# Mixture-of-experts FFN on one core: short last row blocks as float32 column groups, and a preamble in two chains

## The chip, the cores and the metric

One core of one Trainium2 chip runs the kernel. The metric is the time of one execution on the device, in microseconds; lower is better. Three runs of the kernel before took 217.95 us in the median (217.33 to 218.16).

## The reference

```python
def ffn_block(x, cond, q_right, gate, router_w, router_b, w1, b1, w2, b2):
    # r: x rotated by two normalised quaternions, one from cond and one from q_right,
    # and scaled by gate, column by column of the 4 x 64 quaternion parts
    r = hamilton(normalise(cond), hamilton(x * gate, conj(normalise(q_right))))
    logits = r @ router_w + router_b                    # (2048, 8)
    top1 = argmax(softmax(logits))
    out = zeros_like(r)
    for i in range(8):
        h = r @ w1[i] + b1[i]                           # 256 -> 2048
        a, g = split(h, 2)
        y = (a * sigmoid(g)) @ w2[i] + b2[i]            # 1024 -> 256
        out = out + where(top1 == i, y, 0)
    return x + out                                      # x: 8 x 256 tokens of 256 values, float32
```

The gate is constant along the sequence, so that the transform over tokens and its inverse cancel. Each token goes through one expert only. The kernel sorts the tokens by expert and computes each expert on its own tokens.

## The kernel before

**Tiles.** A tile is one expert with up to 512 of its tokens; up to three spare tiles take what is over 512 (none is used with these inputs). A tile is up to four blocks of 128 tokens. `SIZES` (L39) are the widths that the first product can have; each tile takes the smallest that holds its tokens, as a number in a table of control words, `ctrl`, which the kernel itself computes. The second product always computes whole blocks of 128 rows: two, three or four.

**Numbers.** Products are done in a faster 32-bit form, `fp32r`. Each operand is split into a high and a low part (ScalarE copies the high part, VectorE subtracts it from the value), and three products stand for one: high by high, high by low, low by high.

**The preamble.** TensorE turns x block by block (L912), ScalarE and VectorE copy the turned blocks out (L463, L656). VectorE builds the rotation matrix from the quaternions (L588 to L644). The logits are one product in four column groups of 32 columns (L929), with the router turned by the same rotation; ScalarE adds the bias (L485), TensorE turns them back (L949), VectorE finds each token's expert, its rank within the expert and from that its slot (L686 to L721). The counts over partitions are two small products on TensorE (L957, L958). Tables of one-hots (L723, L727) and 16 small products (L968) turn slots into lists of indices: `g_idx` for gathers and `s_idx` for scatters. Between these, TensorE rotates x (L941), ScalarE copies the rotated rows out (L491) and writes them to `x_rows` in DRAM in four DMAs of its own (L495). Then GpSimd gathers the first tile's rows, block by block (L363).

**Filler products** (`keep_warm`, L870, bf16; `keep_warm_long`, L875, float32) stand in places of the preamble where TensorE would otherwise have nothing to do. **Visits** are jumps to a place of TensorE's program that comes later and back.

**A tile.** TensorE turns the gathered rows (L987) at the end of the tile before; ScalarE and VectorE split them (L512, L759) and the tile's w1 in four units (L472, L665). The first product (L1029 to L1034) goes through eight pairs of 128 columns, g then a, in a ring of three pairs of PSUM banks. ScalarE makes the sigmoid (L524), VectorE the gated value into `u32` (L766, a ring of four) and sets `pair_free`, ScalarE and VectorE split that (L530, L772). The second product (L1049 to L1051) takes the blocks from the last to the first, each with 8 x 3 products of 256 columns, as soon as `u_lo_done` says that a part is there; it also waits for `w2_split`. VectorE adds the result to x + b2 in the next tile, after its third pair (L793), for the last tile at once (L801, L806). w2 is split after the third and fifth pair (L481, L670), in tile 0 ahead of them.

**Queues.** SyncE loads x, then w1 and w2 of the tile to come, each when its buffer has been split (L299 and L303). GpSimd issues, per tile and in this order, four gathers for the next tile, four scatters of the tile before and four fetches of x for the next one (L402 to L420).

## Time and profile before

| | us |
|---|---|
| median of three runs | 217.95 |
| profiled execution | 217.55 |
| its span, first to last instruction | 215.8 |
| start of the first expert product | 38.79 |
| TensorE busy | 205.6 |
| VectorE busy | 159.1 |
| ScalarE busy | 121.8 |
| GpSimd busy | 124.6 |
| bytes moved by DMA | 41.26 MB |

Busy times overlap, so that they don't add up. A timeline row gives the start, the duration, the engine, the line of the kernel, the operation with its tile and operands, how many instructions were merged, and in brackets the idle time before them with what ended it. The granted clock is given as a share of TensorE's full speed.

### The profile page before, as it was taken

How to read it: one execution, taken by the hardware profiler on the slowest of the kernel's cores; microseconds unless marked ns; L12 is line 12 of the kernel's file. 1: busy time of each engine (PE TensorE's matmuls, PEld its weight loads, DVE VectorE, ACT ScalarE, POOL GpSimd, SP SyncE). 2: the span in 40 equal slices, each digit the busy share in tenths (PEclk: the TensorE clock that was granted, in tenths of full speed). 3: DMA queues.
4: the chain of work that ended last, by engine and by line, in shares of the span. 5: the costliest groups of instructions: out<-in, count | busy, mean ns of one | idle time of the engine just before them, and what ended most of it. 6: DMA issues, size and time to landing. Idle time of an engine off the chain costs nothing.

```text
span 215.8 us, 4313 instructions
## 1 busy us (share of the span) xinstructions
PE 205.6 (95%) x1500; PEld 191.2 (89%) x1502; DVE 159.1 (74%) x307; ACT 121.8 (56%) x204; POOL 124.6 (58%) x146
## 2 busy tenths in 40 slices
PE   6986998899999999999999999999999999999992
PEld 3756843799999999999999999999999999999991
DVE  6826984877835999298969879994898469874960
ACT  2333692365916666386684958483949185745620
POOL 5000038776730788558878787887487818730751
PEclk9999999999999999999999999999999999999998
DMA  4995523799757173976499559837835692720011
GB/s 140 368 402 186 219 82 91 257 274 380 220 131 307 46 234 71 314 196 204 109 289 288 186 114 362 295 91 184 355 114 180 178 313 70 248 49 0 24 39 36
DMA packets 16964, 41.26 MB, mean 191 GB/s; under 512 B 2856, under 2 KB 11177, under 8 KB 14762
## 3 DMA queue, kind: packets, MB, share of 16 engines
q1 hardware_dynamic: 11490, 28.32, 36.7%
q0 software_dynamic: 4512, 10.50, 19.4%
q10 hardware_dynamic: 936, 2.17, 2.6%
q14 instruction: 19, 0.16, 0.2%
q8 instruction: 7, 0.11, 0.2%
HBM read 36.78 MB, written 6.03 MB: 198 GB/s over the span
## 4 chain that ended last, share of the span: by engine, by line
PE 67%; POOL 14%; issue 8%; DVE 5%; DMA 3%; ACT 1%; DVEq 0%; ACTq 0%; POOLq 0%
PE y_ps L1049 7%; PE y_ps L1051 7%; PE y_ps L1050 7%; PE g_ps L1029 5%; PE g_ps L1034 5%; PE g_ps L1030 5%; POOL out_dram L384 5%; PE a_ps L1029 5%; PE a_ps L1034 5%; PE a_ps L1030 5%; POOL y_out L375 5%; PE y_ps L870 3%; PE y_ps L875 3%; DMA xg<-x_rows,g_idx 3%; POOL xg L363 3%
## 5 line engine op out<-in xcount | busy, mean ns | idle before, releaser
L384 POOL DMA_INDIRECT out_dram<-y_out,s_idx x30 | 44.0, 1466 | 41.2 <-DVE y_out L793 30.4
L524 ACT ACTIVATE arena<-g_ps,b_t 128x384 f32<-128x384 f32 (+1 forms) x64 | 34.4, 538 | 48.2 <-PE g_ps L1034 48.2
L766 DVE SCALAR_TENSOR_TENSOR arena<-a_ps,b_t,arena 128x384 f32<-128x384 f32 (+1 forms) x64 | 36.0, 563 | 30.9 <-PE a_ps L1034 28.4
L363 POOL DMA_INDIRECT xg<-x_rows,g_idx x32 | 37.1, 1159 | 37.1 <-DVE g_idx L732 26.5
L1049 PE MATMUL y_ps<-w_hi,u_hi 128*128 128x256 f32 x168 | 48.5, 289 | 0.1
L1050 PE MATMUL y_ps<-w_lo,u_hi 128*128 128x256 f32 x168 | 47.5, 283 | 0.0
L1051 PE MATMUL y_ps<-w_hi,u_lo 128*128 128x256 f32 x168 | 47.5, 283 | 0.0
L375 POOL DMA_INDIRECT y_out<-in_x_dram,g_idx x32 | 40.3, 1259 | 9.8 <-issue 9.8
L665 DVE TENSOR_TENSOR w_lo<-w_raw,w_hi 128x1024 fp32r<-128x1024 f32 x32 | 37.3, 1221 | 4.7 <-DMA xg<-x_rows,g_idx 3.0
L530 ACT ACTIVATE u_hi<-arena 128x384 fp32r<-128x384 f32 (+1 forms) x64 | 30.7, 480 | 16.0 <-DVE arena L766 16.0
L1029 PE MATMUL g_ps<-xr_hi,w_hi 128*128 128x256 f32 (+3 forms) x128 | 37.0, 303 | 0.6 <-ACT xr_hi L512 0.6
L1029 PE MATMUL a_ps<-xr_hi,w_hi 128*128 128x256 f32 (+3 forms) x128 | 36.6, 299 | 0.0
L1030 PE MATMUL g_ps<-xr_hi,w_lo 128*128 128x256 f32 (+3 forms) x128 | 36.5, 299 | 0.0
L1030 PE MATMUL a_ps<-xr_hi,w_lo 128*128 128x256 f32 (+3 forms) x128 | 36.5, 299 | 0.0
L1049 PEld LDWEIGHTS y_ps<-w_hi,u_hi 128*128 128x128 f32 x168 | 32.2, 192 | 0.7 <-DVE u_lo L772 0.4
L772 DVE TENSOR_TENSOR u_lo<-arena,u_hi 128x384 fp32r<-128x384 f32 (+1 forms) x64 | 31.9, 499 | 1.2 <-ACT u_hi L530 0.3
L1050 PEld LDWEIGHTS y_ps<-w_lo,u_hi 128*128 128x128 f32 x168 | 32.2, 192 | 0.0
L1051 PEld LDWEIGHTS y_ps<-w_hi,u_lo 128*128 128x128 f32 x168 | 32.2, 192 | 0.0
L472 ACT ACTIVATE w_hi<-w_raw 128x1024 fp32r<-128x1024 f32 x32 | 31.2, 1057 | 0.5 <-ACT arena L491 0.5
L1034 PE MATMUL g_ps<-xr_lo,w_hi 128*128 128x256 f32 (+3 forms) x128 | 28.1, 300 | 0.0
L1034 PE MATMUL a_ps<-xr_lo,w_hi 128*128 128x256 f32 (+3 forms) x128 | 27.9, 299 | 0.0
L1029 PEld LDWEIGHTS g_ps<-xr_hi,w_hi 128*128 128x128 f32 x128 | 24.2, 189 | 1.3 <-issue 1.1
(150 smaller groups left out, 298.3 us busy)
## 6 DMA issues: line engine op xcount, KB each, us to landing
w_raw<-in_L_ffn_w_dram SPq DMA_DIRECT2D x16, 1024.0 KB, 8.9
w_raw<-in_L_ffn_w_dram SPq DMA_DIRECT2D x16, 512.0 KB, 5.0
arena<-in_x_dram SPq DMA_DIRECT2D x4, 512.0 KB, 6.2
x_rows<-arena ACTq DMA_DIRECT2D x4, 512.0 KB, 3.0
b_all<-in_L_ffn_b_dram SPq DMA_DIRECT2D x1, 1024.0 KB, 4.9
xg<-x_rows,g_idx POOLq DMA_INDIRECT x32, 7.1
y_out<-in_x_dram,g_idx POOLq DMA_INDIRECT x32, 4.5
out_dram<-y_out,s_idx POOLq DMA_INDIRECT x30
```

The costliest lines, as they stand in the source:

```text
L363: nc.gpsimd.indirect_dma_start(out=xg[:, s * DIM:(s + 1) * DIM], out_offset=None, in_=x_rows, in_offset=bass.IndirectOffsetOnAxis(ap=g_idx ...
L375: nc.gpsimd.indirect_dma_start(out=y_out[i % YB][:, s * DIM:(s + 1) * DIM], out_offset=None, in_=x_flat, in_offset=bass.IndirectOffsetOnAx ...
L384: nc.gpsimd.indirect_dma_start(out=out_flat, out_offset=bass.IndirectOffsetOnAxis(ap=s_idx[:, i * NSUB + s:i * NSUB + s + 1], axis=0), in_ ...
L524: nc.scalar.activation(sig[:, c % SIG_RING, 0:n], pair[c % RING][1][:, 0:n], ACT.Sigmoid, bias=b1_t[:, bass.ds(e * (2 * NC) + (NC + c), 1) ...
L665: V.tensor_tensor(unit_of(w1_lo, u), raw_unit(u), unit_of(w1_hi[:, :].bitcast(F32), u), ALU.subtract)\
L766: V.scalar_tensor_tensor(u32[:, c % (8 - SIG_RING), 0:n], pair[c % RING][0][:, 0:n], b1_t[:, bass.ds(e * (2 * NC) + c, 1)], sig[:, c % SIG ...
L1029: T.matmul(dst, w_part(w1_hi, k), xh, start=(k == 0), stop=False)
L1030: T.matmul(dst, w_part(w1_lo, k), xh, start=False, stop=False)
L1034: last = T.matmul(dst, w_part(w1_hi, k), xr_lo[:, k * ITEM:k * ITEM + n], start=False, stop=(k == KH - 1))
L1049: T.matmul(dst, u_hi[:, uv], w2_hi[:, wv], start=first, stop=False)
L1050: T.matmul(dst, u_hi[:, uv], w2_lo[:, wv], start=False, stop=False)
L1051: last = T.matmul(dst, u_lo[:, uv], w2_hi[:, wv], start=False, stop=final)
```

## The change

**Row blocks.** `SIZES` becomes (192, 256, 288, 320, 352, 512): 192 is new and 384 goes. Where the last block of a size holds 32 or 64 tokens (192, 288, 320), it is computed in float32 directly from `u32` and a whole, unsplit copy of w2, in column groups: the eight parts of the hidden dimension are dealt out to two groups of 64 or four groups of 32 columns of the array, each of which gathers its own partial sum. VectorE adds the groups afterwards, one small addition after the other, chosen by a branch on the tile's size. The first product is at least 256 wide. ScalarE and VectorE work on 256, 288, 320, 384 or 512 columns instead of whole blocks. `u32` now holds all eight parts and moves to the memory of the turned x. The whole w2 is a new load of SyncE, 1 MB per tile, behind the next tile's w1 (behind b2 for tile 0, and last of all for tile 7).

**Preamble.** The logits come in two halves, both before any rotation. A table of the spare tiles' places is made by GpSimd from the counts while VectorE computes the slots; the indices of the eight fixed tiles come first, those of the spare tiles after them in a second set of small products. The rotated rows are written by SyncE in eight DMAs of two row blocks. Half of w2 for tile 0 is loaded after them. The w2 split and the fourth w1 split of tile 0 go behind column pairs. Filler products become fewer, and the visits stand elsewhere. b1 and the gate are loaded by the other queue than before.

```diff
-    SIZES = (256, 288, 320, 352, 384, 512)
+    SIZES = (192, 256, 288, 320, 352, 512)
     BLOCKS = [(size + P - 1) // P for size in SIZES]
+    PARTS = {size: (size // P, size % P) for size in SIZES if size % P in (32, 64)}
...
+            def load_w2_whole(e):
+
+                if e > 0:
+                    sp.wait_ge(w2_whole_loaded, 16 * e)
+                    sp.wait_ge(mm2_done, e)
+                sp.dma_start(w2_whole, w2[e].rearrange("(c p) d -> p c d", p=P)).then_inc(w2_whole_loaded, 16)
...
+                if 1 < i < NE:
+                    load_w2_whole(i - 1)
...
-            for h in range(W2U):
-                load_w2(0, h)
-
+            x_rows_v = x_rows.rearrange("(p n) d -> p n d", p=P)
+            load_w2(0, 0)
+            for b in range(NB // 2):
+                sp.wait_ge(x_rot_done, b + 1)
+                sp.dma_start(x_rows_v[:, 2 * b:2 * b + 2, :], x_rot[:, 2 * b:2 * b + 2, :]).then_inc(x_rows_written, 16)
+            load_w2(0, 1)
             for s in range(NSUB):
                 sp.wait_ge(gathered[s], 16)
             sp.dma_start(b2_all[:, :], b2.rearrange("e d -> (e d)").partition_broadcast(P)).then_inc(b2_loaded, 16)
+            load_w2_whole(0)
             for e in range(1, NE):
                 load_tile(e, e)
+            load_w2_whole(NE - 1)
...
+            for m in range(SPARE):
+                last = G.tensor_single_scalar(over[:, m * NE:(m + 1) * NE], cnt, float((m + 1) * ITEM), ALU.is_gt)
+            link(last)
+            link(G.tensor_tensor(til, over[:, 0:NE], over[:, NE:2 * NE], ALU.add))
...
+            for half in (4 * NB, 2 * NB):
+                link(G.tensor_tensor(of_token[:, 0:half], of_token[:, 0:half], of_token[:, half:2 * half], ALU.add))
+            link(G.tensor_tensor(moved[:, :], of_token[:, 0:NB], of_token[:, NB:2 * NB], ALU.add))
+            pool.sem_inc(moved_ready, 1)
...
-            w2_hi_part(0)
...
-                if b % 2 == 1:
-                    act.wait_ge(x_rot_done, b + 1)
-                    act.dma_start(x_rows_v[:, 2 * b - 2:2 * b + 2, :], x_rot[:, 2 * b - 2:2 * b + 2, :])\
-                        .then_inc(x_rows_written, 16)
...
-            link(V.tensor_reduce(til, over, AX.X, ALU.add))
-            link(V.tensor_tensor_scan(spare_end, ones[:, 0:NE], til, 0.0, ALU.mult, ALU.add))
-            link(V.tensor_tensor(spare_from, spare_end, til, ALU.subtract))
-            link(V.scalar_tensor_tensor(delta, spare_from, float(ITEM), spare_at[:, :], ALU.mult, ALU.add))
-            link(V.scalar_tensor_tensor(ahead_en, pos_en, float(ITEM), delta.unsqueeze(2).to_broadcast([P, NE, NB]),
-                                        ALU.is_ge, ALU.mult))
-            link(V.tensor_tensor(pos[:, :], pos[:, :], ahead[:, :], ALU.add))
...
+            def add_parts(i, word, sizes_here):
+
+                def of_sizes(left):
+                    if not left:
+                        dve.sem_inc(dve_chain, more)
+                        return
+                    s, wide = PARTS[left[0]]
+                    with dve.If(f_size(word) == SIZES.index(left[0])):
+                        rows = y_out[i % YB][0:wide, s * DIM:(s + 1) * DIM]
+                        for g in range(1, P // wide):
+                            link(V.tensor_tensor(rows, y_ps[1][g * wide:(g + 1) * wide, PLACE[s] * DIM:(PLACE[s] + 1) * DIM],
+                                                 rows, ALU.add))
+                        if P // wide - 1 < more:
+                            dve.sem_inc(dve_chain, more + 1 - P // wide)
+                    with dve.Else():
+                        count[0] = start
+                        of_sizes(left[1:])
+
+                start = count[0]
+                more = max(P // wide for _, wide in PARTS.values()) - 1
+                of_sizes(sizes_here)
...
-                if i == 0:
-                    w1_lo_part(0, 3)
-                    w2_lo_part(0)
-                    dve.wait_ge(b2_loaded, 16)
-                elif i < NE:
+                if 0 < i < NE:
...
+                    if c == 1 and i == 0:
+                        w1_lo_part(0, 3)
                     if c == 2 and 0 < i < NE:
-                        add_rows(i - 1)
-                    if c == 4 and 0 < i < NE:
+                        add_rows(i - 1, word_before)
+                    if c == 4 and i < NE:
                         w2_lo_part(i)
                     if c == 4 and i + 1 < NE:
...
+            visit(1)
             pe.wait_ge(still_set, 1)
-            keep_warm(early_ps, 3)
-            visit(1)
+            keep_warm(early_ps, 5)
...
-            keep_warm(early_ps, 8)
-            visit(2)
+            keep_warm(early_ps, 5)
...
+            def logits(half):
+
+                for k in range(KH):
+                    tokens = x_t[:, k, half * 8 * P:(half + 1) * 8 * P].rearrange("p (j a t) -> p a j t", j=2, a=GROUPS)
+                    for a in range(GROUPS):
+                        last = T.matmul(xk_ps[half][a * COLS:(a + 1) * COLS, half * 2 * P:(half + 1) * 2 * P],
+                                        wr_rot[:, k * COLS:(k + 1) * COLS], tokens[:, a],
+                                        start=(k == 0), stop=(k == KH - 1))
+                last.then_inc(logits_t_ready, 1)
 
             pe.wait_ge(wr_ready, 1)
-            pe.wait_ge(x_t_done, 6)
-            pe.wait_ge(x_t_done_v, 2)
-            for k in range(KH):
-                for g in range(GROUPS):
-                    last = T.matmul(xk_ps[0][g * COLS:(g + 1) * COLS, :], wr_rot[:, k * COLS:(k + 1) * COLS],
-                                    x_t[:, k, g * 512:(g + 1) * 512], start=(k == 0), stop=(k == KH - 1))
-            last.then_inc(logits_t_ready, 1)
-            visit(3)
+            pe.wait_ge(x_t_done, 4)
+            logits(0)
+            pe.wait_ge(x_t_done, 7)
+            pe.wait_ge(x_t_done_v, 1)
+            logits(1)
...
+            for g in range(NB // GROUPS):
+                if g == 2:
+                    visit(3)
+                pe.wait_ge(logits_t_done, g // 2 + 1)
+                last = T.transpose(late_ps[:, g * P:(g + 1) * P], logits_t[:, g * P:(g + 1) * P], ident[:, :])
+            last.then_inc(logits_ready, 1)
+
             pe.wait_ge(rot_ready, KH)
-            rotate_blocks(0)
-            pe.wait_ge(logits_t_done, 1)
-            for j in range(NB // GROUPS):
-                last = T.transpose(late_ps[:, j * P:(j + 1) * P], logits_t[:, j * P:(j + 1) * P], ident[:, :])
-            last.then_inc(logits_ready, 1)
-
-            for b in range(1, 3):
+            for b in range(2):
                 rotate_blocks(b)
-            visit(4)
-            pe.wait_ge(consts_ready, 8)
+            pe.wait_ge(consts_ready, CONSTS)
...
+            for b in range(2, NB // 2):
                 rotate_blocks(b)
-
-            visit(5)
+                if b == 5:
+                    visit(4)
+            pe.wait_ge(b1_loaded, 16)
+            T.transpose(early_ps[:, 0:P], b1_rows[:, :], ident[:, :]).then_inc(b1_turned, 1)
+
+            landing(1)
...
             pe.wait_ge(b1_t_done, 1)
-            keep_warm(late_ps, 3)
             pe.wait_ge(q_oh_ready, 1)
             for n in range(NB):
                 pe.wait_ge(slots_ready, n + 1)
-                last = T.matmul(early_ps[:, 0:TS], slot_oh[:, n, :], q_oh[:, n * TS:(n + 1) * TS],
+                last = T.matmul(early_ps[:, 0:FX], slot_oh[:, n, :], q_oh[:, n * FX:(n + 1) * FX],
                                 start=(n == 0), stop=(n == NB - 1))
-                if n < NB - 2:
-                    keep_warm(late_ps, 1)
             last.then_inc(idx_summed, 1)
-            visit(6)
+            visit(5)
             pe.wait_ge(still32_set, 1)
-            keep_warm_long(late_ps, 5)
+            pe.wait_ge(q_oh_spare_ready, 1)
+            pe.wait_ge(x_rot_done, NB // 2)
+            for n in range(NB):
+                last = T.matmul(turn_ps[0][:, 0:TS - FX], slot_oh[:, n, :], q_oh_spare[:, n * (TS - FX):(n + 1) * (TS - FX)],
+                                start=(n == 0), stop=(n == NB - 1))
+            last.then_inc(idx_spare_summed, 1)
+            keep_warm_long(late_ps, 2)
 
             pe.wait_ge(ctrl_ready, 1)
             last_tile = load_last(pe)
             next_word = pe.alloc_register("next_word")
             pe.reg_load(next_word, ctrl[0:1, 1:2])
+            visit(6)
+            keep_warm_long(late_ps, 2)
...
-                            keep_warm_long(late_ps, (1, 2, 0)[s])
+                            keep_warm_long(late_ps, (1, 1, 0)[s])
...
+            def part_block(size, at1, at2, at16, done=None):
+
+                s, wide = PARTS[size]
+                groups = P // wide
+                pe.wait_ge(w2_whole_loaded, at16)
+                for c in range(NC):
+                    pe.wait_ge(pair_free[c], at2 if c >= CARRIED else at1)
+                    g = c % groups
+                    last = T.matmul(y_ps[1][g * wide:(g + 1) * wide, PLACE[s] * DIM:(PLACE[s] + 1) * DIM],
+                                    u32[:, c, s * P:s * P + wide], w2_whole[:, c],
+                                    start=c < groups, stop=c >= NC - groups)
+                if done is not None:
+                    last.then_inc(done, 1)
...
-                with pe.If(f_size(word) >= BLOCKS.index(4)):
-                    row_blocks((3,), at1)
-                with pe.If(f_size(word) >= BLOCKS.index(3)):
+                with pe.If(f_size(word) >= SIZES.index(352)):
+                    with pe.If(f_size(word) >= BLOCKS.index(4)):
+                        row_blocks((3,), at1)
+                        landing(6)
                     row_blocks((2,), at1)
-                row_blocks((1,), at1, done=outer_done)
+                with pe.Else():
+                    with pe.If(f_size(word) == SIZES.index(320)):
+                        part_block(320, at1, at2, at16)
+                    with pe.If(f_size(word) == SIZES.index(288)):
+                        part_block(288, at1, at2, at16)
+                with pe.If(f_size(word) == SIZES.index(192)):
+                    part_block(192, at1, at2, at16, done=outer_done)
+                with pe.Else():
+                    row_blocks((1,), at1, done=outer_done)
                 row_blocks((0,), at1, done=mm2_done)
```

Left out of the diff: `if_width` (a chain of branches over the five widths in place of `if_blocks`), the places of buffers and semaphores, the second set of small products' one-hots on VectorE (after the indices of the fixed tiles), and the evictions of the logits in two halves.

## Rows read from the trace of the kernel before

**Rows 1.** The page, sections 1 and 2.

```profile
PE 205.6 (95%) x1500; PEld 191.2 (89%) x1502; DVE 159.1 (74%) x307; ACT 121.8 (56%) x204; POOL 124.6 (58%) x146
...
PE   6986998899999999999999999999999999999992
...
PEclk9999999999999999999999999999999999999998
```

**Rows 2.** Busy time by stage; after POOL: granted clock, DMA share, GB/s.

```profile
core 0: us, PE busy (x) PEld busy (x) DVE busy (x) ACT busy (x) POOL busy (x), PEclk, DMA share, GB/s
...
87.40:105.60 18.20, 18.20 (x151) 17.79 (x150) 13.89 (x25) 12.49 (x23) 11.84 (x10) 1.00 0.71 225
105.60:123.90 18.30, 18.29 (x152) 17.91 (x151) 15.63 (x27) 12.52 (x23) 14.95 (x12) 1.00 0.76 233
```

**Rows 3.** TensorE's timeline in the preamble: start, duration, operation, idle before.

```profile
13.49 1.92 PE L929 MATMUL a_ps<-x_t,wr_rot 128*32 128x512 f32 x16 [0.77 <-DVE x_t L656]
...
20.44 0.17 PE L957 MATMUL g_ps<-in_row,lower 128*128 128x8 bf16 x1 [1.72 <-issue]
...
29.31 4.56 PE L875 MATMUL y_ps<-still 128*128 128x512 f32 x10
...
36.13 1.88 PE L875 MATMUL y_ps<-still 128*128 128x512 f32 x4
37.85 0.27 PE L987 MATMUL a_ps<-ident,xg 128*128 128x128 f32 x1
...
38.79 0.38 PE L1029 MATMUL g_ps<-xr_hi,w_hi 128*128 128x320 f32 x1 [0.56 <-ACT xr_hi L512]
```

**Rows 4.** VectorE's timeline in the preamble.

```profile
16.97 0.29 DVE L686 TENSOR_REDUCE mx<-y_ps 128x16 f32<-128x128 f32 x1 [3.56 <-PE y_ps L949]
...
20.75 0.17 DVE L702 TENSOR_TENSOR sm<-g_ps,sm 128x8 f32<-128x8 f32 x1 [1.08 <-PE g_ps L958]
...
22.59 0.29 DVE L714 TENSOR_TENSOR work<-work 128x128 f32<-128x128 f32 x1
...
29.31 0.20 DVE L732 TENSOR_SCALAR g_idx<-y_ps 128x44 int32<-128x44 f32 x1 [0.63 <-PE y_ps L968]
```

**Rows 5.** Last rotation copied out, landing of the writes (L495), first gather.

```profile
25.24 0.60 ACT L491 ACTIVATE arena<-g_ps 128x512 f32<-128x512 f32 x1 [0.19 <-PE g_ps L941]
...
DMA to landing us min/median/max: 2.6/3.0/3.9
...
30.41 1.23 POOL L363 DMA_INDIRECT xg<-x_rows,g_idx  x1 [26.53 <-DVE g_idx L732]
```

**Rows 6.** TensorE's timeline around the ends of tiles 2 to 4.

```profile
105.56 0.30 PE L1029 MATMUL g_ps<-xr_hi,w_hi 128*128 128x256 f32 x1
...
123.91 0.37 PE L1029 MATMUL g_ps<-xr_hi,w_hi 128*128 128x288 f32 x1
...
137.04 0.33 PE L987 MATMUL a_ps<-ident,xg 128*128 128x128 f32 x1 [0.25 <-DMA xg<-x_rows,g_idx]
...
137.67 0.36 PE L1049 MATMUL y_ps<-w_hi,u_hi 128*128 128x256 f32 x1
...
146.74 0.37 PE L1029 MATMUL g_ps<-xr_hi,w_hi 128*128 128x288 f32 x1
```

**Rows 7.** SyncE's w1 issues (tiles 5, 6), their landings, then those of w2 (86:107).

```profile
126.00 0.82 SPq L290 DMA_DIRECT2D w_raw<-in_L_ffn_w_dram  x2
...
146.54 0.81 SPq L290 DMA_DIRECT2D w_raw<-in_L_ffn_w_dram  x2
...
DMA to landing us min/median/max: 6.6/8.5/10.4
...
DMA to landing us min/median/max: 6.2/7.9/9.6
...
DMA to landing us min/median/max: 3.6/4.4/5.1
```

**Rows 8.** GpSimd's timeline: start and one block of its row of issues.

```profile
93.62 1.02 POOL L384 DMA_INDIRECT out_dram<-y_out,s_idx  x1 [3.87 <-DVE y_out L793]
...
129.86 1.02 POOL L363 DMA_INDIRECT xg<-x_rows,g_idx  x1 [0.30 <-issue]
```

**Rows 9.** VectorE's timeline: w1 splits of tile 3, and its last addition.

```profile
102.73 4.69 DVE L665 TENSOR_TENSOR w_lo<-w_raw,w_hi 128x1024 fp32r<-128x1024 f32 x4 [0.46 <-ACT w_hi L472]
...
211.64 0.42 DVE L806 TENSOR_TENSOR y_out<-y_ps,y_out 128x256 f32<-128x256 f32 x1 [2.38 <-PE y_ps L1051]
```

242 lines of the change are left out of this document (158 added, 84 removed).

## Prediction

> **What bounds the kernel now.** I read the page first: TensorE is busy 95% of the span, and the two rows of slices show that only the first three or four and the last are not full [rows 1]. So there are three stretches: the preamble (0 to 38.79 us, where the first expert product starts [rows 3]), the body of eight tiles, and a short tail. The timeline of TensorE in the body shows product behind product with no idle in front, with one exception, 0.25 us at 137.04 [rows 6]. Whatever is taken out of TensorE's work in the body is therefore gained, unless something that now arrives just in time becomes late. The table by stage says what stands close behind: in tile 2 (87.4 to 105.6) VectorE is busy 13.9 of 18.2 us and the DMA share is 0.71 [rows 2]. The timeline of GpSimd shows the other close one: from the scatter at 93.62 on it issues one indirect DMA behind the other, 0.3 us apart, and the gather that TensorE waits for at 137.04 is in that row (its third block is issued at 129.86 and lands 7.1 us later) [rows 8]. The preamble is a chain: logits, routing on VectorE, indices, gather, turn, split.
>
> **Token counts.** The seeded inputs route 308, 336, 181, 195, 258, 268, 327 and 175 tokens. So the last row block holds 64 tokens or fewer in tiles 0, 2 and 7 (two groups of 64 columns) and 32 or fewer in tiles 4 and 5 (four groups of 32). Tiles 1, 3 and 6 keep their full blocks. No count lies between 353 and 384, so that the dropped size costs nothing here.
>
> **Part 1: the last row block.** In tile 4 the second product runs from 137.67 to 146.74, 9.07 us for three blocks of 24 products [rows 6]: 3.02 us a block with the edges, 2.9 without (0.12 us a product). The new block is eight float32 products of 256 columns. The nearest row is the logits product, float32 in four column groups: 16 records of 512 columns, 8 products of two passes each, in 1.92 us [rows 3]. If the groups ran one behind the other, at the rate of the full-width float32 records (ten of 512 columns in 4.56 us, 0.456 each [rows 3]), they would take 7.3 us; so the four groups do run together. Four products of 512 columns are 0.96 us, of 256 columns 0.48; eight in four groups are 0.96 us. In two groups, which no row shows, it is between 1.92 (both groups together, twice the rounds) and 3.65 us (no overlap: 16 passes of 0.228); I take 1.9, since it is the same mechanism. Gain: 1.0 us in tiles 0, 2 and 7, and 1.95 in tiles 4 and 5, 6.9 us in all if nothing is late.
>
> What is late next:
> - *The whole copy of w2.* It is a fourth megabyte a tile on SyncE's queue, issued behind the next tile's w1. For tile 4 that w1 goes out at 126.00 and its second half, issued 0.4 us later, takes 10.4 us to land: 136.8 [rows 7]. The w2 halves, 512 KB each, land 3.6 us after the first issue and 5.1 + 0.4 after it [rows 7]: 1.9 us apart, so that the next 1 MB needs 3.9 us behind the w1 (ends 3.5 and 5.5, the latter with a latency of its own). It lands at 140.7, and TensorE wants it at 137.7: it waits, and tile 4 ends at 140.7 + 1.0 + two full blocks of 2.9 = 147.5 instead of 146.74, where 1.95 us less were to be gained. For tile 5, 146.54 + 0.4 + 9.6 + 3.9 = 160.4, and it is wanted one first product and a turn (137.7 - 123.9 = 13.8 us) after 147.5: no wait. For tile 2 I expect 0 to 1 us. In tile 0 it stands right behind b2 and has over 5 us; in tile 7 nothing else is in flight.
> - *GpSimd's row of issues.* It doesn't move when TensorE gets faster in tiles 2 and 3, so the gather for tile 5 still lands at 137.0 (all relative to the end of tile 1). The 1.0 us of tile 2 becomes a wait there. The new megabyte shares the DMA engines with this gather: 0 to 1 us more, I take 0.3.
> - *VectorE.* At the start of tile 3 it ends the fourth w1 split at 107.4, 1.8 us after TensorE has started [rows 9]; TensorE needs only the first unit then, done at about 104.0, and would start at 104.5 instead of 105.56 [rows 6]. That just holds. The 1 to 3 small adds of the column groups (0.42 us each, the row of the last add [rows 9]) and their links come to 0.6 to 1.7 us in a tile. They stand behind the rows' addition in the next tile, where VectorE waits for TensorE again within two column pairs. Tiles 4 and 5 in return work on 288 columns where it was 384, about 0.1 us less on each of 18 operations. Net nothing on the path.
> - *The tail.* In tile 7 the last add starts at 211.64 [rows 9] and moves with TensorE: 1.0 us is gained.
>
> So of the 6.9 us: tile 0 gives 1.0, tile 2 nothing, tile 4 -0.75 (its wait hides the gather's 0.3), tile 5 1.95, tile 7 1.0. Sum 3.2; ends 0 and 6.9.
>
> **Part 2: the preamble.**
> - *Logits in halves, both before the rotations.* The first half runs while the last x_t copy is made. Behind that copy there are 0.96 us of product instead of 1.92, an eviction of 256 columns instead of 512 (about 0.45 for 0.69), and then the turn at once, where the first rotation (1.09 us) stood in between. VectorE started on them at 16.97 [rows 4]; I get 15.35, 1.6 us earlier. The visit of far code between the two pairs of turns could take up to what the sequencer lost at the visit before the ranks, 1.4 us (below).
> - *Ranks.* The count products started at 20.44 after 1.72 us in which TensorE waited for nothing but its own issue, and VectorE waited 1.08 us for them [rows 3, 4]. The visit in front of them goes away: 1.08 us.
> - *VectorE's chain* up to the indices loses seven operations on tables (0.29 us for each of two of 128 columns [rows 4], 0.2 for small ones, links included 1.55 us) and 0.24 us of the smaller one-hot; it takes on about 0.55. The rest is GpSimd's chain, on an engine that is idle until 30.41 [rows 5]: some 12 operations in about 4 us, done before the 16 one-hots are. Gain 1.2. Indices at 29.31 - 3.9 = 25.4.
> - *Row writes.* The last rotation was evicted at 25.84, issued, and landed 3.0 us later [rows 5], near 29.2; the indices were done at 29.5. The two paths ended together, so the shorter index chain alone would give 0.3 us. The writes' path now: turns done 15.3, eight rotations of 0.89 us, 0.4 for the ranks, 22.8, eviction 23.4, SyncE's issue, landing (2.6 to 3.9) at 26.8. Part of a code visit between rotations 5 and 6 may show; I put 0.3 us. SyncE has only w1 and half of w2 for tile 0 queued ahead, which are long landed. GpSimd started 0.9 us after the indices; it starts then at about 28.0 for 30.41: 2.4 us. The writes, not the indices, are last.
> - *Gather to first product.* Unchanged, but for one filler product less before the third turn (two float32 ones took 1.72 us [rows 3], so 0.86 less). The third block should have landed 3 to 4 us after its issue, so that I count 0.5.
> - *Moves at no cost:* the fourth w1 split and the w2 split of tile 0 go behind the first column pairs. TensorE needs them 10 and 14 us into the tile, and they are done after 6 and 12. This holds SyncE's next w1 back to about 6 us into the tile, but its queue is busy until then with b2 and the whole w2.
>
> Preamble: 2.9 us; ends 1.0 (both visits show in full) and 4.4 (neither, full filler gain, indices and writes together).
>
> **Sum.** 2.9 + 3.2 = 6.1 us. The profiled execution took 217.55 us for a span of 215.8; the median is 217.95. The gain is taken off the median: 217.95 - 6.1 = 211.8.
>
> **A rule weighed against the trace.** Two w1 halves, 2 MB, land 10.8 us after the first issue [rows 7], and that price carries the wait of tile 4. The Trainium skill, "DMA: Bandwidth & Descriptors", section on the anatomy of one DMA, fits a transfer by 2.0 us plus its bytes over 436 GB/s. By that, an estimate from the page for 3 MB is 9.2 us, the whole w2 would be there 2.5 us before it is wanted, and rival A holds. The row speaks against it; the gathers run beside these loads.
>
> **Rivals.**
> - *A, nothing is late* (15%). The whole w2 needs no more than 11 us from w1's issue, and the gather comes earlier. For it: the DMA share in tile 2 is 0.71, so there is room. Against it: 10.4 us for w1 alone. 217.95 - 2.9 - 6.9 = 208.1.
> - *B, the body gives nothing but tiles 0 and 7* (17%): tile 5 meets the same wait as tile 4, or a jump over more code on ScalarE or VectorE costs it. 217.95 - 2.9 - 2.0 + 0.5 = 213.6.
> - *C, the clock* (6%). Most of the filler products between 25 and 31 us go, and TensorE has only tiny products there; the granted clock is full in all slices but the last now [rows 1]. If it falls to the lower of its two levels for 7 us of the first product (half of it; no row says how long), 3.5 us are lost: 211.8 + 3.5 = 215.3. The Trainium skill, "TensorE: Matmul & The Clock Gate", on the gate's oscillation, says that gaps bring the slow clock back; the trace shows no such gap yet, and four to six long fillers remain.
> - *D, slower: SyncE's queue becomes the bound* (10%). Tiles 2 and 3 run at a DMA share of over 0.7 [rows 2]; 1 MB in 18 us adds 0.2 or more. If gathers and weights hold each other up and the whole w2 lands 17 us after w1's issue instead of 14.7, tiles 2, 4 and 5 wait 3.5, 5.3 and 3.3 us, and the later gathers add some 2: 14 against 6.9 + 2.9, near 222. It decides from about 15.6 us on, where both sides are 9.8.
> - *E, the groups of 64 don't overlap* (5%, the change doesn't do what it says): 3.65 us for 2.9, 0.75 more instead of 1.0 less in three tiles, and if neither do those of 32, 3.75 us more in all: 217.95 - 2.9 + 3.75 = 218.8.
>
> **Chances and range.** The forecast has 47%. Faster by over 0.5% (about what a measurement of this kernel can tell) holds for it, A, B and C, less a little for misjudged preambles: 0.83. Within 0.5%: 0.07, mostly E. Slower: 0.10, D. The range 207.5 to 216.0 takes in A, B and C and leaves out D and E.
>
> **What the new profile would show.** Right: the first expert product at about 35.9; part blocks of 1.0 and 1.9 us; in tile 4 the first product of the part block idle for a DMA of w2 for 2 to 3.5 us, none in tile 5; a wait of 1 us or more at the turn for tile 5; full clock. Wrong: float32 part products one after the other at over 0.4 us each; GpSimd's first gather still near 30, which would say that the writes or visits didn't move; idle in front of every part block (D); half clock at the first product (C).

## The result, and the profile of the changed kernel

| | kernel before | changed kernel |
|---|---|---|
| median (range) | 218.06 us (217.33 to 220.13) | 232.26 us (229.3 to 234.13) |
| profiled execution, span | 217.55, 215.8 us | 233.85, 232.1 us |
| mean granted clock of TensorE | 0.995 | 0.951 |

The ratio is 1.053, 95% interval 1.040 to 1.066: **slower**, where 211.8 us (207.5 to 216.0) had been predicted. The executions of a kernel fall into a faster and a slower group, and ratios compare the faster ones alone; the profiled execution of the changed kernel is one of its slower ones (the two faster took 229.3 and 230.67 us), so that its 16.3 us over the span of the kernel before are more than the ratio says (about 11.6 us).

The page of the changed kernel, sections 1 to 3, beside [rows 1]:

```profile
PE 205.9 (89%) x1471; PEld 186.0 (80%) x1472; DVE 156.4 (67%) x317; ACT 119.2 (51%) x206; POOL 122.8 (53%) x163
...
PE   7999679999699999959998499999959999999880
...
PEclk9999979999989999997999979999985999999998
DMA  5965726999359457997599749854996178815100
...
q14 instruction: 34, 0.27, 0.4%
```

TensorE is busy for as long as before (205.9 against 205.6 us) in a longer span. Its row of slices has dips all along the body, and the clock has them too, in the same slice or one behind. The last line is new to this document: packets of the kind "instruction", by which the engines fetch their program, here 8 KB each. There are 34 on this queue; the kernel before has 19.

By tile (the changed kernel, each stretch from one first expert product to the next; columns as in [rows 2]):

```profile
62.23:88.80 26.57, 26.53 (x172) 26.23 (x173) 21.74 (x30) 15.85 (x25) 14.22 (x10) 0.94 0.57 193
88.80:110.74 21.94, 19.06 (x142) 16.57 (x140) 12.30 (x24) 11.00 (x22) 14.88 (x14) 0.92 0.90 256
110.74:133.53 22.79, 18.66 (x151) 18.02 (x151) 15.97 (x28) 13.86 (x25) 15.86 (x14) 1.00 0.81 248
133.53:156.40 22.87, 22.82 (x167) 21.33 (x167) 16.57 (x27) 13.27 (x24) 12.64 (x11) 0.93 0.73 231
156.40:182.57 26.17, 23.45 (x167) 21.51 (x166) 17.61 (x30) 13.16 (x23) 16.80 (x15) 0.87 0.75 229
```

Tile 2 takes 21.9 us where it took 18.2, tile 3 22.8 for 18.3, tile 5 26.2 for 22.8. Two things are seen: idle time of TensorE (2.9, 4.1 and 2.7 us), and a granted clock under 1.00 in four of the five. The preamble, in return, is 1.5 us shorter (first product at 37.32, before 38.79). The difference of the two spans, 16.3 us, is the sum over these stages (the table behind the experiments has all of them).

**Where the idle time is from.** TensorE's timeline of the changed kernel, the long idles of the body and the part blocks (last bracket: idle before the row, and what ended it):

```profile
52.35 1.95 PE L1196 MATMUL y_ps<-arena,x_t 128*64 128x256 f32 x16
...
62.23 0.43 PE L1162 MATMUL g_ps<-xr_hi,w_hi 128*128 128x352 f32 x1 [2.00 <-DVE w_lo L743]
...
103.65 3.62 PE L1196 MATMUL y_ps<-arena,x_t 128*64 128x256 f32 x16 [1.56 <-DMA arena<-in_L_ffn_w_dram]
...
133.53 0.40 PE L1162 MATMUL g_ps<-xr_hi,w_hi 128*128 128x288 f32 x1 [3.11 <-DVE w_lo L743]
...
148.86 1.71 PE L1196 MATMUL y_ps<-arena,x_t 128*32 128x256 f32 x16
...
170.38 0.32 PE L1120 MATMUL a_ps<-ident,xg 128*128 128x128 f32 x1 [1.13 <-DVE x_t L852]
...
172.66 1.93 PE L1196 MATMUL y_ps<-arena,x_t 128*32 128x256 f32 x16 [1.41 <-DMA arena<-in_L_ffn_w_dram]
```

There are three kinds of wait: for VectorE's w1 split at a border between tiles, for VectorE's gating at a turn, and for the whole w2. The first kind can be followed. The groups of VectorE's x rests and ScalarE's x copies in the changed kernel:

```profile
L845 DVE TENSOR_TENSOR xr_lo<-a_ps,xr_hi 128x256 fp32r<-128x256 f32 (+3 forms) x8 | 3.8, 474 | 32.6 <-issue 16.5 <-ACT xr_hi L592 16.1
L592 ACT ACTIVATE xr_hi<-a_ps 128x256 fp32r<-128x256 f32 (+3 forms) x8 | 3.4, 423 | 23.4 <-issue 15.8 <-PE a_ps L1120 7.5
```

and the same two in the kernel before:

```profile
L759 DVE TENSOR_TENSOR xr_lo<-a_ps,xr_hi 128x384 fp32r<-128x384 f32 (+1 forms) x8 | 4.1, 507 | 2.7 <-ACT xr_hi L512 2.0 <-issue 0.7
L512 ACT ACTIVATE xr_hi<-a_ps 128x384 fp32r<-128x384 f32 (+1 forms) x8 | 3.6, 448 | 5.8 <-PE a_ps L987 4.6 <-issue 1.0
```

In both, these are the first instructions of a tile's body, behind a jump over the bodies that are not taken. "Issue" means that the engine waited for nothing that the profile shows. Idle time put down to issue goes from 0.7 to 16.5 us on VectorE and from 1.0 to 15.8 us on ScalarE. At the border from tile 3 to tile 4 (VectorE and ScalarE in the changed kernel):

```profile
125.19 0.43 DVE L858 TENSOR_TENSOR u_lo<-x_t,u_hi 128x256 fp32r<-128x256 f32 x1 [0.15 <-ACT u_hi L610]
131.52 0.46 DVE L845 TENSOR_TENSOR xr_lo<-a_ps,xr_hi 128x288 fp32r<-128x288 f32 x1 [5.91 <-issue]
...
125.82 0.41 ACT L592 ACTIVATE xr_hi<-g_ps 128x288 fp32r<-128x288 f32 x1
129.90 3.90 ACT L557 ACTIVATE w_hi<-w_raw 128x1024 fp32r<-128x1024 f32 x4 [3.67 <-issue]
```

In stretches of 0.25 us, the DMA view of the same kernel shows instruction packets at 128.00, 129.25 and 131.50, and none between. The one of 129.25:

```profile
q14 instruction: 1, 0.01, 8.8%
```

In finer stretches these packets start at 128.20, 129.47 and 131.54, and each takes 0.3 to 0.4 us. ScalarE starts at 129.90, 1.3 us after the first is in, and VectorE at 131.52, 1.7 us after the second; the third starts only when VectorE is at work again, so that it didn't release it. At the other four borders with a stall, too, the engine starts 1.3 to 1.9 us after the last packet before it. In the kernel before, the border from tile 3 to 4 has its two packets at 121.50 and 121.75, while both engines are already at work on their splits. So an engine with all its data ready stands still until some time after a piece of its program has come. Which packet belongs to which engine, and what happens between packet and start, the profile doesn't show.

A stall of 3.3 us or more on at least one of the two engines stands at the five borders with four or more bodies between the two taken ones (0 to 1, 2 to 3, 3 to 4, 4 to 5, 5 to 6: the tiles take bodies 2, 3, 0, 0, 1, 1, 3, 0 of five) and at neither of the two others (1 to 2, 6 to 7). The count of bodies is a rough measure: at the border from 4 to 5 VectorE stalls (3.33 us) and ScalarE doesn't.

### The profile page after: what moved, and what is told of

Same layout as the page of the kernel before. It is cut to its first block and busy times, and to the rows that moved or that the text cites. A ratio compares the mean times of both kernels' runs of the same rounds, so it can differ in the third digit from the quotient of the medians.

```text
span 232.1 us, 4377 instructions
## 1 busy us (share of the span) xinstructions
PE 205.9 (89%) x1471; PEld 186.0 (80%) x1472; DVE 156.4 (67%) x317; ACT 119.2 (51%) x206; POOL 122.8 (53%) x163
## 5 line engine op out<-in xcount | busy, mean ns | idle before, releaser
L469 POOL DMA_INDIRECT out_dram<-y_out,s_idx x30 | 36.3, 1211 | 64.1 <-DVE y_out L903 52.6
L604 ACT ACTIVATE arena<-g_ps,b_t 128x256 f32<-128x256 f32 (+3 forms) x64 | 32.7, 510 | 33.7 <-PE g_ps L1167 33.5
L852 DVE SCALAR_TENSOR_TENSOR x_t<-a_ps,b_t,arena 128x256 f32<-128x256 f32 (+3 forms) x64 | 33.7, 529 | 22.9 <-PE a_ps L1167 18.2
L448 POOL DMA_INDIRECT xg<-x_rows,g_idx x32 | 37.7, 1179 | 14.7 <-issue 9.1
L610 ACT ACTIVATE u_hi<-x_t 128x256 fp32r<-128x256 f32 (+3 forms) x64 | 29.1, 454 | 29.6 <-DVE x_t L852 29.5
L1182 PE MATMUL y_ps<-w_hi,u_hi 128*128 128x256 f32 x128 | 38.4, 300 | 0.4 <-issue 0.3
L1163 PE MATMUL a_ps<-xr_hi,w_lo 128*128 128x256 f32 (+3 forms) x128 | 37.3, 304 | 0.0
L1183 PE MATMUL y_ps<-w_lo,u_hi 128*128 128x256 f32 x128 | 37.0, 289 | 0.0
L1184 PE MATMUL y_ps<-w_hi,u_lo 128*128 128x256 f32 x128 | 37.0, 289 | 0.0
L858 DVE TENSOR_TENSOR u_lo<-x_t,u_hi 128x256 fp32r<-128x256 f32 (+3 forms) x64 | 29.8, 466 | 1.3 <-ACT u_hi L610 0.5
L1182 PEld LDWEIGHTS y_ps<-w_hi,u_hi 128*128 128x128 f32 x128 | 25.4, 198 | 4.0 <-issue 3.2
L845 DVE TENSOR_TENSOR xr_lo<-a_ps,xr_hi 128x256 fp32r<-128x256 f32 (+3 forms) x8 | 3.8, 474 | 32.6 <-issue 16.5
L1183 PEld LDWEIGHTS y_ps<-w_lo,u_hi 128*128 128x128 f32 x128 | 25.4, 199 | 0.0
```

The lines of the kernel that those rows point to most:

```text
L448: nc.gpsimd.indirect_dma_start(out=xg[:, s * DIM:(s + 1) * DIM], out_offset=None, in_=x_rows, in_offset=bass.IndirectOffsetOnAxis(ap=g_idx ...
L469: nc.gpsimd.indirect_dma_start(out=out_flat, out_offset=bass.IndirectOffsetOnAxis(ap=s_idx[:, i * NSUB + s:i * NSUB + s + 1], axis=0), in_ ...
L852: V.scalar_tensor_tensor(u32[:, c, 0:n], pair[c % RING][0][:, 0:n], b1_t[:, bass.ds(e * (2 * NC) + c, 1)], sig[:, c % SIG_RING, 0:n], ALU. ...
L858: V.tensor_tensor(u_lo[:, at:at + n], u32[:, c, 0:n], u_hi[:, at:at + n].bitcast(F32), ALU.subtract).then_inc(u_lo_done[c], 1)
L1163: T.matmul(dst, w_part(w1_lo, k), xh, start=False, stop=False)
L1182: T.matmul(dst, u_hi[:, uv], w2_hi[:, wv], start=first, stop=False)
```

## The experiments

The kernels ran in six sets, each on one chip and with the kernel before in it, which took 218 us in two of the sets and 225 to 227 us in the four others. So a ratio is read against the kernel before of its own set, named as "beside 227" and so on. Kernels of different sets are compared with that reserve.

**Three bodies** instead of five on ScalarE and VectorE, the rest as changed. The edit also gives up the narrower widths, since these bodies work on whole blocks:

```diff
-  if_width(act, this_word(act, word_at), lambda n: gate_tile(e, e, n))
+  if_blocks(act, this_word(act, word_at), lambda blocks: gate_tile(e, e, blocks * P))
```

and likewise on VectorE. 

> The changed kernel, but ScalarE and VectorE branch between three bodies a tile (2, 3 or 4 whole blocks, as before the change) instead of five widths; the part blocks, the whole w2 and the preamble stay. Theory 1 (jumps): in the changed kernel ScalarE sat idle 15.8 us ahead of its first split and VectorE 16.5 us, with nothing but their own issue as the reason, and only at the tile borders where four or more bodies lie between the end of one tile's code and the start of the next tile's (tiles 0 to 1, 2 to 3, 3 to 4, 4 to 5, 5 to 6), never where one lies between (1 to 2, 6 to 7). With three bodies at most three are jumped over, so these waits fall below 1 us each, the clock stays up in the body, and the time is 211 to 217. Theory 2 (the load of the whole w2 is the bound): the part blocks waited for it in two tiles only, 1.6 and 1.4 us, but if the jumps only hid it, the time stays above 225. Theory 3 (clock: fewer filler products leave TensorE at its lower level): the granted clock in tiles 1 to 7 stays broken into low stretches and the time stays above 226.

Measured: 229.59 us beside 227.11, ratio 1.010 (1.002 to 1.019). The stalls at the borders are gone (1.1 and 1.0 us of issue in front of the x rests and copies for 16.5 and 15.8, and 22 instruction packets for 34), as the first theory had it. But no gain is left, so that the jumps are not the whole cause.

**Five bodies on the kernel before**, of its own three widths (`if_width` with `-(-n // P) * P`), three times. 

> The kernel before with one edit: ScalarE and VectorE branch over five bodies a tile as in the change, with the widths of before (256, 384, 384, 384, 512). No work is added on the path. Theory 1: idle by issue of 3 to 7 us ahead of the first split at the same five borders; a tile's second product of 5.8 to 8.6 us covers a part of each, so 8 to 14 us are lost: 226 to 232. VectorE's bodies are a little shorter than in the change (no adds of column groups), so the lower end is likelier. Theories 2 and 3: 218, no change, since no load, no filler product and no part block is touched.

Measured: 227.06 us beside 227.11, 0.997 (0.992 to 1.002).

> Five bodies on the kernel before, a second time. It gave 0.997 beside a kernel before of 227 us, although its trace shows stalls for code at three borders. If that before of 227 us already held stalls of its own, then beside a before of 218 us the five bodies cost what their stalls in front of TensorE add up to (1.7 to 1.8 us at two borders and what the clock loses behind them): 1.015 to 1.03. If they are harmless as long as no part blocks and no whole w2 are there: 1.00.

Measured: 226.76 us beside 226.72, 0.998 (0.994 to 1.002).

> Five bodies on the kernel before, once more, for a before of 218 us. Beside one of 225 to 227 us the ratio was 0.997 and 0.998, but tile by tile the traces show tiles 2, 3 and 7 longer by 1.9, 2 to 3 and 2.1 us than before's best, and no pause of 7 us in tile 3, which the trace of before has there. If the bodies' cost was masked by that pause, the ratio is 1.02 to 1.035 beside a before of 218 us. If the bodies are harmless alone: 1.00 there too. Beside a before of 226 us: 0.995 to 1.00 by both.

Measured: 227.16 us beside 227.46, 0.999 (0.995 to 1.004). Before took 227 us again, so that the question of this run isn't answered. The stalls are there (second run; groups of the x rests and copies):

```profile
L771 DVE TENSOR_TENSOR xr_lo<-a_ps,xr_hi 128x384 fp32r<-128x384 f32 (+1 forms) x8 | 4.1, 507 | 12.0 <-ACT xr_hi L524 7.4 <-issue 4.6
L524 ACT ACTIVATE xr_hi<-a_ps 128x384 fp32r<-128x384 f32 (+1 forms) x8 | 3.6, 449 | 12.2 <-issue 7.4 <-PE a_ps L999 4.7
```

but their sum is under half of that in the changed kernel (4.6 and 7.4 us for 16.5 and 15.8), and there are 29 packets for 34. VectorE's bodies in the changed kernel also hold the part additions; why ScalarE's stalls are longer there stays open.

**The new preamble alone**: no part blocks, no whole w2, three bodies. 

> The new preamble alone: three bodies, no part blocks (every last block is a full one in split form) and no load of the whole w2; the result is the same. Theory 1: the body is that of before and the preamble gives what its trace shows, the first expert product at 37.3 instead of 38.8, so 216.5 (215 to 217.5). Theory 3: the fillers that were taken out leave the clock low at the first product, as the changed kernel's 0.70 between 30 and 35 us suggests, and tile 0 costs 1 to 3 us more: 218 to 220.

Measured: 230.63 us beside 227.11, 1.014 (1.006 to 1.023). The first product starts 2 us earlier (36.9), but tile 0 takes 31.0 us for 24.0, with pauses of 2.0 to 4.7 us on ScalarE and VectorE in it, of the kind described below.

**No whole w2 after tile 0's**, three bodies: 

> As three_bodies, but the whole w2 is loaded for tile 0 only and the part blocks don't wait for a later one (they use the w2 of expert 0 in tiles 2, 4, 5 and 7, a part of the computation that is changed). It prices the load: my prediction had a wait of 2.7 us in tile 4 and up to 1 us in tile 2, with 7 MB more on SyncE's queue. If that was right, this is 2.5 to 4 us faster than three_bodies; if the load is free once the jumps are gone, less than 1 us; if it is the main cause (theory 2), over 8 us.

Measured: 229.44 us beside 227.11, 0.996 (0.990 to 1.003). Tile by tile the waits in front of the part blocks of tiles 2 and 4 are gone (18.3 and 22.4 us). By the ratios the load costs 1.4% (1.010 against 0.996), as expected; but the medians with and without it are alike (229.59 and 229.44 us), so that this price is weakly shown.

**Before and after once more**, in one set. 

> The kernel before, unchanged, for a trace of it beside the others of this call. If jumps over more bodies of code cost nothing (theory: code), there should be no row of ScalarE's second x copy or VectorE's rest with more than 1 us of idle put down to issue; if such stalls come on this chip in the kernel before too, its span will be above 215.8 us by about their sum, which would say that they are a matter of the chip or of its memory traffic and not of the number of bodies. Ratio 1.00 either way.

Measured: 225.82 us beside 225.49, 1.001 (0.997 to 1.005). No stall at a border, but a pause in the middle of tile 3, in which VectorE and ScalarE stand for 4 to 5 us each, one behind the other, and TensorE works in short pieces, while GpSimd goes on with its row of issues. ("Remote" is what the profile says where it finds no instruction that released the engine.) VectorE, ScalarE and TensorE in this trace:

```profile
120.67 0.48 DVE L766 SCALAR_TENSOR_TENSOR arena<-a_ps,b_t,arena 128x256 f32<-128x256 f32 x1 [4.24 <-remote]
...
123.52 0.47 ACT L524 ACTIVATE arena<-g_ps,b_t 128x256 f32<-128x256 f32 x1 [4.94 <-remote]
...
120.63 0.40 PE L1034 MATMUL g_ps<-xr_lo,w_hi 128*128 128x256 f32 x2 [0.92 <-issue]
```

Tile 3 takes 25.6 us here and 18.3 in the trace of [rows 6]. There is no instruction packet in this pause: it is another thing than the stalls at the borders.

> The changed kernel, unchanged, beside its halves. The last call gave 1.010 for it with three bodies, 1.014 for the new preamble alone and 1.00 for five bodies on the old kernel. If the parts add up (no interaction), 1.01 to 1.02; if the five bodies cost only together with the part blocks and the whole w2 (more code and more bulk transfers in the queues at once), 1.04 to 1.06, with stalls put down to issue of 3 us or more at five of seven borders between tiles.

Measured: 236.27 us beside 225.49, 1.047 (1.038 to 1.056): the halves don't add up to it, the five bodies cost more together with the rest. This agrees with the second expectation.

**Part blocks alone**: old preamble, fillers and split order; part blocks and whole w2; three bodies. 

> The old preamble, its fillers and its order of splits, with the part blocks and the whole w2 of the change, and three bodies on ScalarE and VectorE. By the first call the preamble is what costs (1.014 alone against 1.010 with the parts): then this one is faster than before, 0.985 to 0.99 (the two waits for the whole w2 take back half of 6.9 us). If the whole w2's megabyte and the row of GpSimd's gathers eat what the blocks save: 1.00.

Measured: 228.42 us beside 225.49, 1.016 (1.010 to 1.021). Neither expectation: the parts cost time.

**Tile 0's splits ahead of its pairs again**, otherwise the new preamble alone:

```diff
+            w2_hi_part(0)        # ScalarE, ahead of tile 0
+                if i == 0:       # VectorE, ahead of the pairs
+                    w1_lo_part(0, 3)
+                    w2_lo_part(0)
```

> The new preamble alone, but with the fourth split of w1 and both splits of w2 of tile 0 back ahead of its first column pair, as in the kernel before. If the move of these splits into tile 0 costs the 5 us that tile 0's first product takes longer (20 to 22 us instead of 16 to 17), that product is back at 16 to 17 us and the ratio at 1.00 or below, against 1.014 without this edit. If it is the thinned fillers and the clock, or the traffic of loads at that moment, the product stays at 20 us or over, and the ratio at 1.01 to 1.02.

Measured: 223.75 us beside 225.49, 0.990 (0.981 to 0.999); tile 0 takes 26.6 us, not 31.0. The two kernels ran in different sets.

> The new preamble alone, three bodies, with tile 0's splits ahead of its pairs, a second time. It gave 0.990 beside a before of 225.5 us. If the preamble brings what was worked out (2 to 3 us) wherever it runs: 0.985 to 0.99. If its gain was only a pause less, as the pauses come in some of the runs there, 1.00 beside a before of 218 us.

Measured: 225.54 us beside 226.72, 0.997 (0.991 to 1.002), between the two expectations; tile 0 at 25.6 us.

**Five bodies on one engine only**, otherwise as changed. 

> The changed kernel with five bodies (of the three widths of before) on ScalarE only and three on VectorE. The changed kernel ran at 1.047 and with three bodies on both at 1.010. If the jumps over more code cost engine by engine, the stalls on VectorE's x rests (3 to 7 us in the trace of the changed kernel) go and those of ScalarE (3.7 to 5.9 us) stay; VectorE's second pair of fetches stood behind ScalarE's, so that the ratio is between: 1.02 to 1.035.

Measured: 228.81 us beside 217.91, 1.052 (1.046 to 1.059).

> The counterpart: five bodies on VectorE only, three on ScalarE. VectorE's program is the longer one (1550 rows against 958), and it is VectorE that TensorE waits for at the border from tile 3 to 4 (3.11 us). Code fetches engine by engine: 1.02 to 1.04, with issue stalls on the x rests alone. If the two engines' fetches only cost where they meet, both this and the other are at 1.01.

Measured: 230.89 us beside 217.91, 1.062 (1.055 to 1.068). The ratios are above what was expected, with a kernel before of 218 us here; in us both lie between three bodies and five (227 to 230 and 232 to 236). The groups show it engine by engine. Five on VectorE only:

```profile
L845 DVE TENSOR_TENSOR xr_lo<-a_ps,xr_hi 128x256 fp32r<-128x256 f32 (+3 forms) x8 | 3.8, 474 | 21.4 <-issue 15.2 <-ACT xr_hi L592 6.2
L592 ACT ACTIVATE xr_hi<-a_ps 128x384 fp32r<-128x384 f32 (+1 forms) x8 | 3.6, 448 | 7.8 <-PE a_ps L1120 6.7 <-issue 1.0
```

Five on ScalarE only:

```profile
L845 DVE TENSOR_TENSOR xr_lo<-a_ps,xr_hi 128x384 fp32r<-128x384 f32 (+1 forms) x8 | 4.1, 508 | 17.2 <-ACT xr_hi L592 17.2
L592 ACT ACTIVATE xr_hi<-a_ps 128x384 fp32r<-128x384 f32 (+1 forms) x8 | 3.6, 449 | 18.9 <-issue 12.8 <-PE a_ps L1120 6.0
```

The issue time goes with the engine that has the bodies, 15.2 us on one and 12.8 on the other; where ScalarE has it, VectorE waits behind it (17.2 us).

**Five bodies, whole w2 loaded once.** 

> The changed kernel with all its bodies, but the whole w2 is loaded once and not for each tile, so that a seventh of the loads is gone (the part blocks of tiles 1 to 7 multiply with expert 0's w2: this kernel leaves out the loads of the other experts' whole w2). If the code fetches are slow because they stand among bulk transfers (five bodies cost nothing on the old kernel, where stalls were 2.6 to 3.9 us, and 8 us here, where they were 3.3 to 7.1), the stalls fall to 2.5 to 4 us and the ratio to 1.01 to 1.02. If they are the price of the longer code alone, the stalls stay at 4 to 7 us and only the waits for w2 (3 to 4 us in all) go: 1.03.

Measured: 231.29 us beside 217.91, 1.059 (1.054 to 1.064). The stalls at the borders were 2.5 to 5.3 us on ScalarE and 3.2 to 6.0 on VectorE, against 3.7 to 5.9 and 3.3 to 7.1, so most of each is there without the seven loads. Neither expected ratio came. Beside the changed kernel with early splits, of the same set (the next run), it is 3.0 us faster, and that kernel's waits for the whole w2 are 2.23 and 2.91 us.

**The changed kernel with tile 0's splits early.** 

> The changed kernel, whole, with only tile 0's last w1 split and w2 splits back ahead of its first pair. In the new preamble alone this edit took the ratio from 1.014 to 0.990. If what it saves is in tile 0's first product (20 us back to 17) and adds to the rest: 1.047 less 0.02 to 0.024, so 1.023 to 1.03. If tile 0's splits only cost by chance of a pause there, no change: 1.04 to 1.05.

Measured: 234.33 us beside 217.91, 1.076 (1.070 to 1.082). A miss: tile 0 took 25.0 us here, just as long as in the changed kernel beside 218 (24.9). There the place of the splits is worth nothing. Their 4 to 5 us showed only where tile 0 met pauses; the second trace of the changed kernel, with its 29.1 us, has such pauses too.

**Preamble with early splits, part blocks, three bodies.** 

> The same with the part blocks and the whole w2 of the change, three bodies. It tells their net worth: if the waits for the whole w2 in tiles 2 and 4 (1.7 to 2 us each) and the clock behind them eat the 6.9 us: 0.99 to 1.00, or 1.01 where the table by tile of the parts with the old preamble holds (tiles 2 and 4 each 3 us longer); against the changed kernel with these splits (1.076) the two extra bodies would then be worth 0.07.

Measured: 227.36 us beside 226.72, 1.003 (0.998 to 1.008), and two w2 waits. TensorE in this kernel:

```profile
104.04 1.95 PE L1198 MATMUL y_ps<-arena,x_t 128*64 128x256 f32 x16 [2.04 <-DMA arena<-in_L_ffn_w_dram]
...
145.51 1.13 PE L1198 MATMUL y_ps<-arena,x_t 128*32 128x256 f32 x16 [2.18 <-DMA arena<-in_L_ffn_w_dram]
...
168.66 0.32 PE L1122 MATMUL a_ps<-ident,xg 128*128 128x128 f32 x1 [1.87 <-DVE x_t L853]
```

**The same, the whole w2 ahead of w1 in SyncE's queue:**

```diff
 def load_tile(i, e):
+    if 1 < i < NE:
+        load_w2_whole(i - 1)
     for u in range(W1U):
         sp.wait_ge(w1_split[u], i)
     for k in range(KH):
         load_w1(e, k)
-    if 1 < i < NE:
-        load_w2_whole(i - 1)
```

> The same with the whole w2 of a tile issued ahead of the next tile's w1 instead of behind it. It can go out at the tile's start, when the DMA engines are nearly idle (30 to 130 GB/s behind a border). If the queue order is what makes TensorE wait in tiles 2, 4 and 5, the waits of 1.3 to 2.5 us are gone and the ratio falls by 0.015 to 0.03 below the same kernel with the old order, to 0.97 to 0.98 at best. If it only moves the lateness to w1's splits or to the gathers, the ratio stays within 0.005 of the other's.

Measured: 225.6 us (222.3 to 228.4, four runs) beside 226.72, no interval.

> New preamble with early splits, part blocks, three bodies, the whole w2 ahead of w1, once more. Beside a before of 218 us: its table by tile, less the pause in tile 3, comes to 36.5 + 25 + 25.0 + 18.3 + 19 + 22.3 + 23.9 + 25.9 + 21.6 = 217.5 against 215.8 for before: 1.005 to 1.01. If the preamble and the part blocks are worth what was predicted once the queue's order and the extra bodies are out of the way, 0.97 to 0.98. Beside a before of 226 us: 0.985 to 0.995 by both.

Measured: 226.05 us beside 227.46, 0.989 (0.982 to 0.997). Both waits for w2 are gone (tiles 2 and 4 take 18.3 and 22.3 us for 19.8 and 25.0), and this version is faster than the kernel before, by 1.1%, where that takes 227 us. Where before takes 218 it wasn't run. What is left in it is VectorE; first run, VectorE and then TensorE in tile 5:

```profile
158.98 1.33 DVE L886 TENSOR_TENSOR y_out<-y_ps,y_out 32x256 f32<-32x256 f32 x3 [0.33 <-DVE y_out L907]
160.72 0.62 DVE L853 SCALAR_TENSOR_TENSOR x_t<-a_ps,b_t,arena 128x384 f32<-128x384 f32 x1 [0.41 <-issue]
...
166.10 0.32 PE L1122 MATMUL a_ps<-ident,xg 128*128 128x128 f32 x1 [1.88 <-DVE x_t L853]
```

The three small additions and what lies around them hold VectorE for 2.07 us (0.33 + 1.33 + 0.41), and TensorE waits 1.88 us for it at the next turn.

**By tile**, in us, from the first expert product of one tile to that of the next, tile 7 to the end of the span. "218" marks the traces of the two sets in which the kernel before takes 218 us.

| kernel (profiled execution) | preamble | 0 | 1 | 2 | 3 | 4 | 5 | 6 | 7 |
|---|---|---|---|---|---|---|---|---|---|
| before, 218 | 38.8 | 24.0 | 24.6 | 18.2 | 18.3 | 22.8 | 22.8 | 24.6 | 21.7 |
| before again | 40.4 | 25.6 | 24.6 | 18.2 | 25.6 | 22.9 | 22.8 | 24.5 | 21.8 |
| before, five bodies (second run) | 38.7 | 26.3 | 24.6 | 20.2 | 21.5 | 23.0 | 22.7 | 24.6 | 24.0 |
| new preamble alone | 36.9 | 31.0 | 24.6 | 18.2 | 25.3 | 22.7 | 23.0 | 24.5 | 21.7 |
| the same, early splits | 36.6 | 26.6 | 24.5 | 18.2 | 25.5 | 22.7 | 23.0 | 24.6 | 21.8 |
| changed, three bodies | 36.7 | 29.7 | 25.0 | 19.6 | 20.2 | 24.9 | 23.8 | 25.9 | 21.6 |
| parts alone | 38.4 | 25.5 | 25.0 | 21.4 | 19.5 | 25.8 | 23.8 | 25.7 | 21.5 |
| preamble, early splits, parts | 36.3 | 27.7 | 25.1 | 19.8 | 20.0 | 25.0 | 23.9 | 25.9 | 21.7 |
| the same, w2 first | 36.5 | 25.9 | 25.0 | 18.3 | 23.3 | 22.3 | 23.9 | 25.9 | 21.6 |
| changed, five on ScalarE, 218 | 35.9 | 25.1 | 25.0 | 21.2 | 21.9 | 23.8 | 23.9 | 26.0 | 21.7 |
| changed, five on VectorE, 218 | 36.5 | 23.7 | 25.0 | 21.5 | 21.7 | 22.8 | 26.1 | 25.7 | 23.9 |
| changed, 218 | 37.3 | 24.9 | 26.6 | 21.9 | 22.8 | 22.9 | 26.2 | 25.6 | 23.9 |
| changed, early splits, 218 | 37.3 | 25.0 | 25.0 | 21.9 | 22.8 | 24.0 | 27.2 | 25.7 | 24.0 |
| changed again | 36.0 | 29.1 | 25.1 | 21.0 | 22.9 | 23.0 | 26.7 | 25.7 | 23.8 |

The table splits the 16.3 us of the profiled executions. The preamble gives 1.5 and tile 0 costs 0.9: its products are 1.1 us shorter, as forecast, and the stall at its end takes 2.0. In tiles 1 to 7, the row with parts and three bodies ("preamble, early splits, parts") is longer than before by 0.5 + 1.6 + 1.7 + 2.2 + 1.1 + 1.3 + 0.0 = 8.4 us: the **part blocks**, whatever their products save. The changed kernel is longer than that row by another 1.5 + 2.1 + 2.8 - 2.1 + 2.3 - 0.3 + 2.2 = 8.5 us: the **two extra bodies**. With the two other traces of the changed kernel this term is 6.8 ("changed again") and 9.2 us (early splits), and with five bodies on one engine alone 5.3 (VectorE) and 2.1 (ScalarE). It fits the 8.3 us by which the two ratios beside 225 to 227 differ (1.047 and 1.010; with both intervals, 5.5 to 11). The 2.2 us in tile 7 lie wholly behind the last addition: it starts 17.5 us into the tile in both kernels, and the span ends 4.2 us after it in the kernel before, 6.4 us with five bodies on VectorE and 4.3 with five on ScalarE alone.

The 8.4 sets a trace from beside 227 against one from beside 218; in tiles 1, 2, 4, 5, 6 and 7 the kernel before has the same times in both kinds of set, and tile 3 is the exception. No kernel with three bodies was run beside 218 us. An estimate for one, from the trace with five on ScalarE less its 2.1 us (224.5 - 2.1, and 1.7 from span to time), is 224 us: the extra bodies would then be somewhat over half of the loss there, and the part blocks the rest.

The same table says why five bodies on the kernel before seem to cost nothing: tiles 2, 3 and 7 are 2.0, 3.2 and 2.3 us longer than in the first row, and the pause of 7 us in tile 3 doesn't come. With the pause in one and the stalls in the other, both take 227 us. That this is why the ratio is 1.00 there is argued from one trace of each, not shown beside a kernel before without pauses.

## Why the prediction was wrong

**The preamble: right up to the gather.** Up to there the terms held one by one; of the 2.9 us forecast in all, 1.5 came. The changed kernel's VectorE, ScalarE and GpSimd in the preamble, and its first product:

```profile
15.30 0.29 DVE L761 TENSOR_REDUCE mx<-y_ps 128x16 f32<-128x128 f32 x1 [2.20 <-PE y_ps L1073]
...
25.25 0.19 DVE L810 TENSOR_SCALAR g_idx<-y_ps 128x32 int32<-128x32 f32 x1
...
23.22 0.60 ACT L577 ACTIVATE arena<-g_ps 128x512 f32<-128x512 f32 x1 [0.30 <-PE g_ps L1065]
...
27.20 1.26 POOL L448 DMA_INDIRECT xg<-x_rows,g_idx  x1 [3.69 <-DMA x_rows<-arena]
...
37.32 0.38 PE L1162 MATMUL g_ps<-xr_hi,w_hi 128*128 128x320 f32 x1 [0.51 <-ACT xr_hi L592]
```

Predicted were 15.35 for the logits on VectorE, 25.4 for the indices, 23.4 for the last rotation copied out, 28.0 for the first gather (it waits for the row writes, as said), and 35.9 for the first product. That one is late: from 32 to 34 us the granted clock is 0.50, its lower level (1.2 of 2.4 GHz), and 0.65 on the mean from 34 to 36, so that two long fillers in front of a turn take 1.92 us where four took 1.88 [rows 3] (here rival C's mechanism, in another place than the one it named):

```profile
32.00:34.00 2.00, 2.00 (x5) 0.94 (x4) 0.00 (x0) 0.00 (x0) 1.39 (x2) 0.50 0.24 64
34.00:36.00 2.00, 2.00 (x6) 0.71 (x5) 0.00 (x0) 0.00 (x0) 1.69 (x2) 0.65 0.45 88
```

Ahead of that TensorE had stood for 2.25 us of issue up to 30.76, behind the last code visit. Where the clock held, in the kernel with five bodies on ScalarE, the first product starts at 35.9 us.

**The part block: its size was right, its neighbours weren't.** At full clock it takes 1.95 us in two groups and 1.07 to 1.13 in four, as worked out from [rows 3] (1.9 and 1.0): the column groups do run together, and rival E falls. At the lower clock it takes 3.62 and 1.93 us. But in four groups it is through its parts so soon that it can catch up with VectorE. VectorE and then TensorE in tile 5, with three bodies and early splits:

```profile
170.38 0.60 DVE L853 SCALAR_TENSOR_TENSOR x_t<-a_ps,b_t,arena 128x384 f32<-128x384 f32 x1
...
169.57 1.06 PE L1198 MATMUL y_ps<-arena,x_t 128*32 128x256 f32 x14
171.04 0.62 PE L1198 MATMUL y_ps<-arena,x_t 128*32 128x256 f32 x2 [0.41 <-issue]
```

The last part of `u32` is written until 170.98, and the last product starts at 171.04: the block spans 2.1 us, not 1.07. In tile 4 of the changed kernel it spans 1.71 us at full clock, for the same reason. The prediction took its full 1.95 us of gain there.

**The wait for the whole w2: right in size, in more places than one.** With three bodies w1 is issued at 130.71 and TensorE gets the whole w2 in tile 4 at 145.5, 14.8 us later; 14.7 was the forecast from [rows 7]. The estimate by the Trainium skill, "DMA: Bandwidth & Descriptors", section on the anatomy of one DMA (9.2 us for 3 MB), was far too short here. The page gives its fit for a single DMA issued by GpSimd, and these were three megabytes in SyncE's queue beside gathers; for such a load the measurement decides. But tile 2 waits as well, 2.04 us, where 0 to 1 was put. In the changed kernel, which runs late in tile 4, the waits are in tiles 2 and 5 (1.56 and 1.41 us). The gather that was to swallow tile 2's gain never came last: there was no gain to swallow.

**The step that failed first: "Net nothing on the path"** for VectorE's additions. It took tiles 4 and 5 to work on 288 columns in return and a wait of VectorE to absorb the rest. VectorE has no such slack: in tile 5 of the kernel with w2 first it is busy through all of the 5.0 us from 161.0 to 166.0, ahead of the turn, and TensorE waits for it there. Such waits at the turn are 0.60, 1.22, 0.68 and 1.87 us in tiles 2 to 5 with three bodies and early splits, 4.4 in all; the kernel before has none for VectorE over 0.4 us (row by row it was followed in tile 5 only). In that kernel TensorE is busy for 146.3 of the 161.4 us of tiles 1 to 7, and before for 148.4 of 153.0. So its idle time grows by 10.5 us: 4.4 at the turns, 4.2 for the whole w2, the rest in waits of 0.65 us or less. Its busy time falls by only 2.2 us, where the part products at full clock are 5.5 us shorter than the full blocks. Part of the difference is the clock (0.93 in tile 4) and the block that waits for VectorE. That tiles 1 and 6, which hold no part block, are 0.4 to 1.3 us longer in every kernel with part blocks and three bodies, stays open.

At the end, where 1.0 us was to be gained, tile 7 takes 21.7 us as before: the part block's 2.0 to 2.1 us come behind 0.6 us of issue, against 2.9 for a full block, and the last addition, which waits for TensorE, starts 17.5 us into the tile in both kernels.

**The step that was missing: the code.** Rival B had the mechanism in half a sentence ("a jump over more code on ScalarE or VectorE costs it") at 0.5 us. It cost 8.5 (6.8 to 9.2 by the three traces of the whole change). The prediction counted what each instruction of the new bodies does and not what it takes to reach them: five bodies for three, each with the part additions inside it, so that the jumps at five borders go over four to six bodies (at most three before). Both kernels' pages carry the sign for it (issue in front of the x copies, and the count of instruction packets); 1.0 us over eight tiles had looked like nothing to multiply.

**The clock made it dearer.** The granted clock is 0.50, the lower level, for a stretch behind each of TensorE's waits of 2.00, 1.56, 3.11 and 1.13 us (in tiles 1, 2, 4 and 5): in tile 5, with 2.7 us of idle, it is 0.87 on the mean. An upper estimate from the stretches by tile, (1 - clock) times their length, is 1.6 + 1.8 + 1.6 + 3.4 = 8.4 us, part of which coincides with the idle. In tile 7 it falls only behind the last product (1.00 up to 225.70), which costs nothing. Rival C had it in the first product alone, at 3.5 us. These us are inside the terms above and don't come on top.

Of the signs named in the prediction, the one for the part blocks' size held; the first product came 1.4 us late, tile 5's part block waited where none was to, and the clock wasn't full. The sign of D, idle in front of the part blocks, stood in two of five. Rival D had the side right (slower, 222) and its mechanism in part: w2 landed 14.8 us after w1, not 17. What it lacked were the bodies and VectorE.

## What to carry to other kernels

- A body that is written out once more costs nothing where it is not run, but it moves the next taken one away. Ahead of such a change, count the bodies between two taken ones and look for issue time in front of their first instructions; where it is long, the engine starts late though its data are there (up to 7.1 us here).
- A load that is needed late but can start early goes ahead in the queue of one that is needed later: the same megabyte cost two waits of 2 us behind w1 (three bodies) and none ahead of it.
- A microsecond taken off the busiest engine and put on the next one is a trade, not a gain, if that one has no idle time in the stretch that the busiest waits on.

## What the runs showed of the hardware

- The packets that fetch program on queue 14 are 8 KB here (34 in the changed kernel, 0.27 MB); seven more, on queue 8, are 16 KB each in both kernels. The Trainium skill, "Advanced Engine Details and Errata", section "ISA Cache", has 32 KB for an engine other than TensorE, in two lines of 16 KB; the packets on queue 14 are half a line. The Trainium skill, "CRC Debugging", section "Comparing the Two Runs", names queue 14 as that of the sequencers' instruction refill; the traces agree.
- An engine that jumps over four or more long bodies can stand for 2.5 to 7.1 us, and starts again 1.3 to 1.9 us after the last instruction packet before it. The Trainium skill, "Advanced Engine Details and Errata", section "Control Flow Timing", gives 0.108 us for a compare and branch; the jumps that had to wait for their code took over 20 times that.
- More bodies mean more packets: 19 with three bodies in the kernel before and 29 to 30 with five; in the changed kernel 22 with three on both engines, 26 with five on ScalarE, 29 with five on VectorE and 33 or 34 with five on both.
- In the sets in which the kernel before takes 225 to 227 us, pauses of 2 to 5 us come in the middle of a tile, on VectorE and ScalarE, with little work on TensorE, while GpSimd goes on, in tiles 0 and 3 above all. The one shown above has no instruction packet in it. The traces of the sets with 218 us have none over 2 us. What makes them wasn't found, nor whether they belong to the chip: one chip was used twice, and the kernel before took 225.5 and 227.5 us on it. They hide stalls and make changes look better or worse by some per cent: the two extra bodies on the kernel before looked free beside 227 us, and tile 0's split order looked worth 4 us there and nothing beside 218.
